# Group norm and attention on one core: loads split by columns, last probabilities kept in spent input, buffers moved by 32 bytes

## The chip, the core and the metric

One core of a Trainium2 chip runs the whole program. The time is the device time of that core in microseconds (us), from runs of the same kernel; less is better. The profile is one further execution, recorded by the hardware profiler.

## The reference

The input x has 16 images of 32 x 32 pixels with 512 channels, in float32. For every image (N = 1024 tokens, C = 512):

```
xn   = group_norm(x, 32 groups) * gamma + beta
q, k, v = xn @ wq + bq, xn @ wk + bk, xn @ wv + bv
attn = softmax(q @ k^T * C**-0.5)          # over the 1024 keys
out  = (attn @ v) @ wp + bp + x
```

## The kernel before, in words

**Algebra.** The weights are folded once, in a setup: A stands for wq and wk^T multiplied, M for wv and wp. So q k^T is computed as t against xn with t = A^T xn, and (attn v) wp as attn against v' = xn M. The biases bv, wp and bp make one row, out_bias, which is added to the residual x. Every matmul operand is split into a high and a low part (float32r), and each product is three matmuls: hi x hi, hi x lo, lo x hi (`product`, L780 to L791). Each matmul is 128 x 128 against 512 columns.

**One image on PE** (`image`, L896 to L918): two v tiles (24 matmuls), eight score tiles of the first half of the queries (h = 0, 12 matmuls each, xn stationary and t moving), four t chunks for the second half, six v tiles, eight score tiles of the second half, four output tiles of the first half (24 matmuls each, pt stationary and v moving, L871 to L873), four t chunks of the next image, four output tiles of the second half. The images 1 to 14 are a loop; the first and the last are written out.

**The softmax.** ACT copies a score tile to `score` (L451); DVE keeps a running maximum (top_part, L616); POOL reduces it over partitions (`top`, L334); DVE makes the shift and adds it to the eight tiles (`shifts`, L632); ACT takes the exp in place (L456), then writes the high part pt_hi (`pt_hi_parts`, L464), and DVE the low part pt_lo (`pt_lo_parts`, L637, by the helper at L524). POOL sums the exps (`totals`, L344) and reduces them over partitions (L352); DVE turns them into total_inv. `tile_out` (L652 to L658) scales an output tile and adds x_res, the residual in which POOL has added out_bias (`residual`, L322). For the second half the order is, on ACT, all eight exps (L507) and then pt_hi in four pairs; on DVE, tile_out 0, the eight shifts, tile_out 1 to 3, then pt_lo in pairs (L754 to L762). pt_hi waits at its start until the output tiles of the first half are done (s_o, L461), as these read the old pt.

**The loads.** SP issues all loads of x and of the weights, in the order written. An image of x comes in four quarters of 256 tokens (`load_quarter`, L232). Each quarter goes to one buffer [128, 1024]: partition i*32 + t holds the channels of block i (128 of 512) of token t, for the eight groups j of 32 tokens. The kernel issues one DMA for each i: 32 partitions, eight pieces of 512 bytes each. The first image goes to the free `score` buffer, the others to the two halves of x_blk. DVE transposes a quarter in 32 x 32 blocks to x_t (L533). In the loop a quarter is loaded once the quarter that had the buffer is transposed: quarters 2 and 3 of the next image after the transposes of its quarters 0 and 1. These transposes are placed by the table TRANSPOSED (L226). The rows of wq, wk and wv go to the partitions in the same permuted order (`load_weight`, L247), one DMA for each i, 32 partitions with four pieces of 2 KB. w_p is one DMA over 128 partitions. SP's order at the start: w_q, w_k, four quarters of x, w_v, w_p, three wide bias vectors, two quarters of image 1. ACT's queue loads gamma and beta, four rows with four pieces of 32 elements (128 bytes) each, and bv, four rows of 128 elements (512 bytes): L423 and L425.

**The setup chain behind w_p.** ACT writes wp_hi (L477), POOL wp_lo (L361); with these PE makes M. POOL then takes the root for rstd (L315), which DVE's norm and so xn wait for, and after it sums out_bias (L370 to L379). ACT waits for out_bias (L489) before it enters the first image.

**Addresses.** Buffers lie one after another, each rounded up to 32 bytes. In bytes within a partition: xn_hi 53088, xn_lo 69472, a_hi 85856, a_lo 94048, m_hi 102240, m_lo 110432 (all 32 past a multiple of 64), t_hi 145728, t_lo 153920, v_hi 162112, v_lo 178496, pt_hi 194880, pt_lo 211264 (all multiples of 64).

Of the kernel before, what the change touches and what calls it, by code (L numbers as in the profile page):

```python
# [8 lines left out]
ACT = mybir.ActivationFunctionType  # L9
# [4 lines left out]
P = 128  # L14
BANK = 512
# [4 lines left out]
def group_norm_attention(nc, x, gamma, beta, wq, bq, wk, bk, wv, bv, wp, bp, out):  # L20
# [28 lines left out]
    NQ = 4  # L49
    TQ = N // NQ  # L50
    assert NI == KC and SQ % CG == 0
    x_quarters = x.rearrange("b h w c -> b (h w) c").rearrange("b (q j t) (i r) -> b q i t j r", q=NQ, t=SQ, i=NI)
    out_rows = out.rearrange("b h w c -> b (h w) c").rearrange("b (t p) c -> b p t c", p=P)

    ctx = ExitStack()
    with ctx:
# [48 lines left out]
        with ExitStack() as setup:  # L105
# [3 lines left out]
                                              for n in ("wv_t_lo", "wv_t_hi", "wp_lo", "wp_hi"))  # L109
# [6 lines left out]
        (wq_t_hi, wq_t_lo), (wk_t_hi, wk_t_lo) = ([part[:, :, half * C:(half + 1) * C] for part in (xn_hi, xn_lo)]  # L116
                                                  for half in range(2))
        t_hi = sb("t_hi", [P, KC, BANK], F32R)
        t_lo = sb("t_lo", [P, KC, BANK], F32R)
# [67 lines left out]


        def starts(n, h=0):

            return h == 0 and isinstance(n, int) and n == 0
# [39 lines left out]
        def _(sp):  # L231
            def load_quarter(n, q):  # L232
                for i in range(NI):
                    sp.dma_start(quarter_of(n, q)[i * SQ:(i + 1) * SQ, :].rearrange("t (j r) -> t j r", r=P),  # L234
                                 x_quarters[n, q, i]).then_inc(s_xb[q], 16)

# [10 lines left out]
            def load_weight(w, dst, loaded):  # L247
                for i in range(NI):
                    sp.dma_start(dst[i * SQ:(i + 1) * SQ, :, :],  # L249
                                 w.rearrange("(i k a) n -> i a k n", i=NI, k=KC)[i]).then_inc(loaded, 16)  # L250

# [169 lines left out]
        def _(act):  # L421
# [36 lines left out]
            def pt_hi_parts(n, h, first, end):  # L458
                if first == 0 and end and not starts(n, h):

                    act.wait_ge(s_o, n * NT + h * TH)  # L461
                for m in range(first, end):
                    act.wait_ge(s_p, (n * NH + h) * NT + m + 1)
                    nc.scalar.activation(pt_hi[:, m, :], score[:, m, :], ACT.Copy).then_inc(s_pth, 1)  # L464

# [25 lines left out]
            def image(b, more):  # L491
                hi_part(b, "v", 0, 0)
                hi_part(b, "v", 0, 1)
                scores_out(b, 0)
                for j in range(KC):
                    hi_part(b, "t", 1, j)
                    exps(b, 0, *SHIFTED.get(("t", j), (0, 0)))
                for m in range(2, NT):
                    hi_part(b, "v", 0, m)
                    exps(b, 0, *SHIFTED.get(("v", m), (0, 0)))  # L500
                    pt_hi_parts(b, 0, *SPLIT_UP.get(("v", m), (0, 0)))
                scores_out(b, 1)
                if more:

                    act.wait_ge(s_work, use(b, "s", 1, NT - 1))
                    xn_split(b + 1)
                exps(b, 1, 0, NT)  # L507
                for j in range(KC):
                    pt_hi_parts(b, 1, 2 * j, 2 * j + 2)
                    if more:  # L510
                        hi_part(b + 1, "t", 0, j)
# [10 lines left out]
        def _(dve):  # L522
# [3 lines left out]
            def quarter_transpose(n, q):  # L526
                if q == 0 and not starts(n):

                    dve.wait_ge(s_rv, n * KC)
                dve.wait_ge(s_xb[q], (n + 1) * 16 * NI)  # L530
                blocks = quarter_of(n, q).rearrange("p (j k a) -> p k j a", k=KC, a=SQ)
# [102 lines left out]
            def pt_lo_parts(n, h, first, end):  # L634
                for m in range(first, end):
                    dve.wait_ge(s_pth, (n * NH + h) * NT + m + 1)
                    lo_part(pt_lo[:, m, :], score[:, m, :], pt_hi[:, m, :], s_ptl)  # L637

# [74 lines left out]
            def image(b, more):  # L713
# [41 lines left out]
                tile_shift(b, 1)  # L755
                shifts(b, 1, 0, NT)
                for i in range(1, TH):
                    tile_out(b, i)
                for j in range(KC):
                    pt_lo_parts(b, 1, 2 * j, 2 * j + 2)  # L760
                    if more:
                        split_lo_part(b + 1, "t", 0, j)  # L762
                if more:
                    for k in range(KC):
                        row_part(b + 1, k)
# [13 lines left out]
        def _(pe):  # L779
# [22 lines left out]
            def weight_transpose(u0, w, loaded):  # L802
                pe.wait_ge(loaded, 16 * NI)
                for j in range(KC):
# [50 lines left out]
            def out_tile(n, i, more):  # L855
# [7 lines left out]
                if i == TH - 1 and more:  # L863

                    pe.wait_ge(s_pw_in, n + 2)
                dst = o_ps[i % TH]
                for m in range(NT):
                    if i % TH == 0:
                        pe.wait_ge(s_ptl, (n * NH + h) * NT + m + 1)
                    queries = chunk(i % TH)  # L870
                    nc.tensor.matmul(dst, pt_hi[:, m, queries], v_hi[:, m, :], start=m == 0, stop=False)  # L871
                    nc.tensor.matmul(dst, pt_hi[:, m, queries], v_lo[:, m, :], start=False, stop=False)  # L872
                    last = nc.tensor.matmul(dst, pt_lo[:, m, queries], v_hi[:, m, :], start=False, stop=m == NT - 1)  # L873
                last.then_inc(s_o, 1)

# [71 lines left out]
```

## Time and profile before

| | us |
|---|---|
| median of 3 runs | 2180.49 (2180.29 to 2183.83) |
| the profiled execution, its own time | 2182.63 |
| its span in the profile | 2180.9 |
| PE busy with matmuls | 2153.6 (99% of the span) |
| DVE busy | 1434.9 (66%) |
| POOL busy | 829.6 (38%) |
| ACT busy | 672.7 (31%) |
| PE's first wait, for w_q | 8.4 |

Engines: PE is the matrix engine, DVE the vector engine, ACT the scalar engine, POOL GpSimd, SP the engine that issues DMAs here; SPq is SP's DMA issues. Matmuls overlap each other, so their duration (390 ns) is longer than the distance from one start to the next (227 ns): for the pace of PE the starts are what counts. "idle before" is how long an engine had been idle, with what ended it. Time in which an engine waits costs something only where the chain that ends last runs through it.

### The profile page before, as it was taken

Reading aid. Unit: us, or ns where it says so; the run is one execution under the profiler, and the core shown is the slowest. Engines: PE = TensorE matmul, PEld = TensorE weight load, DVE = VectorE, ACT = ScalarE, POOL = GpSimd, SP = SyncE. Lnnn points to the kernel's source line nnn. Section 1 sums busy time; section 2 is a strip of 40 time slices with the busy share of each in tenths; the row PEclk is TensorE's granted clock in tenths of the full one; section 3 lists DMA queues with packets and bytes.
Section 4 is the critical chain, followed back from the end, with each engine's and each line's share of the span. In section 5 each row is a group of like instructions: output and inputs, shape, how many; then the busy total and the mean of one; then the engine's idle time right before and its main releaser. Section 6 shows DMA issues by size and latency. Waiting matters only on the chain.

```text
span 2180.9 us, 28171 instructions
## 1 busy us (share of the span) xinstructions
PE 2153.6 (99%) x9425; PEld 1762.9 (81%) x9425; DVE 1434.9 (66%) x2280; ACT 672.7 (31%) x1113; POOL 829.6 (38%) x487
## 2 busy tenths in 40 slices
PE   6999999999999999999999999999999999999998
PEld 5788888888888888888888888888888888888886
DVE  6775675856668475774756758576684757748454
ACT  3241332414233132331413324142331323314231
POOL 3344343433433335332443434334333343324433
PEclk9999999999999999999999999999999999999999
DMA  7003021030302103021030210303021030210201
GB/s 169 20 15 102 1 73 43 29 86 0 96 19 58 58 5 101 10 63 53 14 101 0 72 43 29 86 0 96 19 58 58 5 101 10 63 53 10 68 0 59
DMA packets 109259, 106.03 MB, mean 49 GB/s; under 512 B 8492, under 2 KB 74032, under 8 KB 109232
## 3 DMA queue, kind: packets, MB, share of 16 engines
q1 hardware_dynamic: 109184, 105.68, 17.3%
q8 instruction: 15, 0.25, 0.0%
q14 instruction: 12, 0.10, 0.0%
q10 hardware_dynamic: 48, 0.01, 0.0%
HBM read 72.10 MB, written 33.55 MB: 48 GB/s over the span
## 4 chain that ended last, share of the span: by engine, by line
PE 94%; POOL 2%; issue 2%; SPq 1%; DMA 1%; ACT 0%; DVE 0%; POOLq 0%; ACTq 0%; DVEq 0%
PE psum L788 21%; PE psum L790 21%; PE psum L789 21%; PE psum L873 10%; PE psum L871 10%; PE psum L872 10%; SPq L234 1%; DMA w_p<-in_L_conv_wp_dram 1%; POOL total_part L344 0%; POOL bias_part L370 0%; POOL x_res L322 0%; SPq L249 0%; ACT score L456 0%; POOL out_bias L374 0%; PE psum L834 0%
## 5 line engine op out<-in xcount | busy, mean ns | idle before, releaser
L788 PE MATMUL psum<-t_hi,xn_hi 128*128 128x512 f32 x1024 | 406.4, 397 | 1.3 <-DVE v_lo L524 1.3
L790 PE MATMUL psum<-t_hi,xn_lo 128*128 128x512 f32 x1024 | 405.0, 396 | 0.0
L789 PE MATMUL psum<-t_lo,xn_hi 128*128 128x512 f32 x1024 | 405.0, 395 | 0.0
L871 PE MATMUL psum<-v_hi,pt_hi 128*128 128x512 f32 x1024 | 399.1, 390 | 4.5 <-DVE pt_lo L524 4.5
L873 PE MATMUL psum<-v_hi,pt_lo 128*128 128x512 f32 x1024 | 398.6, 389 | 0.0
L872 PE MATMUL psum<-v_lo,pt_hi 128*128 128x512 f32 x1024 | 398.6, 389 | 0.0
L322 POOL TENSOR_TENSOR x_res<-x_res,out_bias 128x512 f32<-128x512 f32 (+1 forms) x144 | 179.7, 1259 | 437.1 <-issue 233.8
L616 DVE TENSOR_TENSOR top_part<-top_part,score 128x512 f32<-128x512 f32 x192 | 169.3, 882 | 254.6 <-ACT score L451 253.1
L451 ACT ACTIVATE score<-psum 128x512 f32<-128x512 f32 x256 | 151.3, 599 | 481.3 <-PE psum L790 481.3
L344 POOL TENSOR_TENSOR total_part<-total_part,score 128x512 f32<-128x512 f32 x192 | 279.4, 1455 | 46.2 <-ACT score L456 31.5
L456 ACT ACTIVATE score<-score 128x512 f32<-128x512 f32 x256 | 157.5, 633 | 293.7 <-DVE score L632 293.7
L524 DVE TENSOR_TENSOR pt_lo<-score,pt_hi 128x512 fp32r<-128x512 f32 x256 | 243.0, 993 | 0.0
L788 PEld LDWEIGHTS psum<-t_hi,xn_hi 128*128 128x128 f32 x1024 | 192.4, 188 | 47.5 <-DVE v_lo L524 1.9
L790 PEld LDWEIGHTS psum<-t_hi,xn_lo 128*128 128x128 f32 x1024 | 192.3, 188 | 46.5
L871 PEld LDWEIGHTS psum<-v_hi,pt_hi 128*128 128x128 f32 x1024 | 192.2, 188 | 46.6 <-DVE pt_lo L524 4.6
L789 PEld LDWEIGHTS psum<-t_lo,xn_hi 128*128 128x128 f32 x1024 | 192.4, 188 | 45.6
L873 PEld LDWEIGHTS psum<-v_hi,pt_lo 128*128 128x128 f32 x1024 | 192.3, 188 | 40.2
L872 PEld LDWEIGHTS psum<-v_lo,pt_hi 128*128 128x128 f32 x1024 | 192.3, 188 | 39.9
L632 DVE TENSOR_TENSOR score<-score,shift 128x512 f32<-128x512 f32 x256 | 217.2, 904 | 1.1
L657 DVE SCALAR_TENSOR_TENSOR x_res<-psum,total_inv,x_res 128x512 f32<-128x512 f32 x128 | 93.6, 746 | 175.1 <-POOL x_res L322 108.9
L788 PE MATMUL psum<-xn_hi,a_hi 128*128 128x512 f32 x512 | 199.9, 390 | 2.7 <-DVE xn_lo L524 2.7
L788 PE MATMUL psum<-m_hi,xn_hi 128*128 128x512 f32 x512 | 200.7, 392 | 0.0
(101 smaller groups left out, 2995.0 us busy)
## 6 DMA issues: line engine op xcount, KB each, us to landing
x_res<-in_x_dram SPq DMA_DIRECT2D x128, 256.0 KB, 2.9
out_dram<-x_res SPq DMA_DIRECT2D x128, 256.0 KB, 2.1
x_blk<-in_x_dram SPq DMA_DIRECT2D x240, 128.0 KB, 2.9
score<-in_x_dram SPq DMA_DIRECT2D x16, 128.0 KB, 7.8
w_q<-in_L_conv_wq_dram SPq DMA_DIRECT2D x4, 256.0 KB, 4.8
w_k<-in_L_conv_wk_dram SPq DMA_DIRECT2D x4, 256.0 KB, 8.0
w_v<-in_L_conv_wv_dram SPq DMA_DIRECT2D x4, 256.0 KB, 8.4
w_p<-in_L_conv_wp_dram SPq DMA_DIRECT2D x1, 1024.0 KB, 11.4
```

What stands on the lines that cost most here:

```text
L322: last = nc.gpsimd.tensor_tensor(at, at, out_bias[:, first:end], ALU.add)
L344: nc.gpsimd.tensor_tensor(total_part[:], score[:, 0, :] if m == 1 else total_part[:], score[:, m, :], ALU.add).then_inc(s_sum, 1)
L456: nc.scalar.activation(score[:, m, :], score[:, m, :], ACT.Exp, scale=SCALE).then_inc(s_p, 1)
L524: nc.vector.tensor_tensor(dst, src, hi.bitcast(FP32), ALU.subtract).then_inc(signal, 1)
L616: nc.vector.tensor_tensor(top_part[:], score[:, 0, :] if m == 1 else top_part[:], score[:, m, :], ALU.max).then_inc(s_mx, 1)
L632: nc.vector.tensor_tensor(score[:, m, :], score[:, m, :], shift[:], ALU.add).then_inc(s_sub, 1)
L788: nc.tensor.matmul(dst, s_hi_, m_hi_, start=n == 0, stop=False)
L789: nc.tensor.matmul(dst, s_hi_, m_lo_, start=False, stop=False)
L790: last = nc.tensor.matmul(dst, s_lo_, m_hi_, start=False, stop=n == len(pairs) - 1)
L871: nc.tensor.matmul(dst, pt_hi[:, m, queries], v_hi[:, m, :], start=m == 0, stop=False)
L872: nc.tensor.matmul(dst, pt_hi[:, m, queries], v_lo[:, m, :], start=False, stop=False)
L873: last = nc.tensor.matmul(dst, pt_lo[:, m, queries], v_hi[:, m, :], start=False, stop=m == NT - 1)
```

## The change

Three things change.

1. `load_quarter` issues one DMA for each group j of 32 tokens (QJ = 8) in place of one for each channel block i: 128 partitions, one piece of 512 bytes each. `load_weight` issues one DMA for each k in place of each i: 128 partitions, one piece of 2 KB each. The semaphore counts that readers wait for follow.
2. A buffer t_offset of 32 bytes is put before t_hi, so t_hi, t_lo, v_hi, v_lo, pt_hi and pt_lo lie 32 bytes further on.
3. In the second half of the last image the probabilities are written over xn_hi and xn_lo, which are no longer needed once the last score product is done; so ACT waits for that product and not for the output tiles of the first half. Exps, shifts, pt_hi and pt_lo go in pairs there, and tile_out 1 to 3 come after pt_lo.

```diff
-    x_quarters = x.rearrange("b h w c -> b (h w) c").rearrange("b (q j t) (i r) -> b q i t j r", q=NQ, t=SQ, i=NI)
+    QJ = TQ // SQ
+    x_quarters = x.rearrange("b h w c -> b (h w) c").rearrange("b (q j t) (i r) -> b q j i t r", q=NQ, t=SQ, i=NI)
...
+        sb("t_offset", [P, 8])
         t_hi = sb("t_hi", [P, KC, BANK], F32R)
...
+        def final_half(n, h):
+            return h == NH - 1 and isinstance(n, int) and n == B - 1
+        def probs(n, h):
+            if final_half(n, h):
+                return [x[:].rearrange("p k (t q) -> p (k t) q", q=BANK) for x in (xn_hi, xn_lo)]
+            return pt_hi, pt_lo
...
             def load_quarter(n, q):
-                for i in range(NI):
-                    sp.dma_start(quarter_of(n, q)[i * SQ:(i + 1) * SQ, :].rearrange("t (j r) -> t j r", r=P),
-                                 x_quarters[n, q, i]).then_inc(s_xb[q], 16)
+                for j in range(QJ):
+                    sp.dma_start(quarter_of(n, q)[:, j * P:(j + 1) * P], x_quarters[n, q, j]).then_inc(s_xb[q], 16)
...
             def load_weight(w, dst, loaded):
-                for i in range(NI):
-                    sp.dma_start(dst[i * SQ:(i + 1) * SQ, :, :],
-                                 w.rearrange("(i k a) n -> i a k n", i=NI, k=KC)[i]).then_inc(loaded, 16)
+                for k in range(KC):
+                    sp.dma_start(dst[:, k, :],
+                                 w.rearrange("(i k a) n -> k i a n", i=NI, k=KC)[k]).then_inc(loaded, 16)
...
             def pt_hi_parts(n, h, first, end):
-                if first == 0 and end and not starts(n, h):
+                if first == 0 and end and final_half(n, h):
+                    act.wait_ge(s_work, use(n, "s", h, NT - 1))
+                elif first == 0 and end and not starts(n, h):
                     act.wait_ge(s_o, n * NT + h * TH)
...
-                exps(b, 1, 0, NT)
+                    exps(b, 1, 0, NT)
                 for j in range(KC):
+                    if not more:
+                        exps(b, 1, 2 * j, 2 * j + 2)
                     pt_hi_parts(b, 1, 2 * j, 2 * j + 2)
...
-                shifts(b, 1, 0, NT)
-                for i in range(1, TH):
-                    tile_out(b, i)
-                for j in range(KC):
-                    pt_lo_parts(b, 1, 2 * j, 2 * j + 2)
-                    if more:
+                if more:
+                    shifts(b, 1, 0, NT)
+                    for i in range(1, TH):
+                        tile_out(b, i)
+                    for j in range(KC):
+                        pt_lo_parts(b, 1, 2 * j, 2 * j + 2)
                         split_lo_part(b + 1, "t", 0, j)
+                else:
+                    shifts(b, 1, 0, 2)
+                    for j in range(KC):
+                        if j < KC - 1:
+                            shifts(b, 1, 2 * j + 2, 2 * j + 4)
+                        pt_lo_parts(b, 1, 2 * j, 2 * j + 2)
+                    for i in range(1, TH):
+                        tile_out(b, i)
```

The output tiles of the last half read `probs(n, h)` in place of pt_hi and pt_lo. The waits for a quarter and for a weight count 16 * QJ and 16 * KC in place of 16 * NI.

## Rows read from the trace of the kernel before

**Rows 1.** Page, part 4: shares of the chain that ended last, by engine.

```profile
PE 94%; POOL 2%; issue 2%; SPq 1%; DMA 1%; ACT 0%; DVE 0%; POOLq 0%; ACTq 0%; DVEq 0%
```

**Rows 2.** PE's timeline, one image: start us, us, engine line op out<-in.

```profile
995.61 0.40 PE L788 MATMUL psum<-t_hi,xn_hi 128*128 128x512 f32 x1
...
1018.01 0.39 PE L788 MATMUL psum<-xn_hi,a_hi 128*128 128x512 f32 x1
...
1028.92 0.39 PE L788 MATMUL psum<-m_hi,xn_hi 128*128 128x512 f32 x1
...
1034.36 0.28 PE L834 MATMUL psum<-mv,group_avg 128*128 128x4 f32 x2
...
1068.11 0.39 PE L871 MATMUL psum<-v_hi,pt_hi 128*128 128x512 f32 x1
...
1089.88 0.39 PE L788 MATMUL psum<-xn_hi,a_hi 128*128 128x512 f32 x1
```

**Rows 3.** PE's groups, shapes kept apart: xcount | busy us, mean ns.

```profile
L788 PE MATMUL psum<-t_hi,xn_hi 128*128 128x512 f32 x1024 | 406.4, 397 | 1.3 <-DVE v_lo L524 1.3
...
L871 PE MATMUL psum<-v_hi,pt_hi 128*128 128x512 f32 x1024 | 399.1, 390 | 4.5 <-DVE pt_lo L524 4.5
```

**Rows 4.** Timelines of ACT, POOL and ACT in the setup.

```profile
31.34 1.15 ACT L477 ACTIVATE wp_hi<-w_p 128x512 fp32r<-128x512 f32 x2 [4.24 <-DMA w_p<-in_L_conv_wp_dram]
...
39.02 1.50 POOL L315 TENSOR_TENSOR rstd<-g_var,minus_half 128x4 f32<-128x4 f32 x1 [1.47 <-DVE g_var L567]
...
72.67 1.08 ACT L439 ACTIVATE v_hi<-psum 128x512 fp32r<-128x512 f32 x2 [10.23 <-POOL out_bias L379]
```

**Rows 5.** The end: timelines of DVE, POOL, PE, then PE's waits.

```profile
2138.84 4.90 DVE L632 TENSOR_TENSOR score<-score,shift 128x512 f32<-128x512 f32 x8
...
2144.45 1.28 POOL L344 TENSOR_TENSOR total_part<-score 128x512 f32<-128x512 f32 x1 [7.17 <-ACT score L456]
...
2149.91 9.26 DVE L524 TENSOR_TENSOR pt_lo<-score,pt_hi 128x512 fp32r<-128x512 f32 x8
...
2173.80 3.76 POOL L322 TENSOR_TENSOR x_res<-x_res,out_bias 128x512 f32<-128x512 f32 x3 [7.70 <-issue]
...
2176.41 0.39 PE L873 MATMUL psum<-v_hi,pt_lo 128*128 128x512 f32 x1
...
PE psum L871 <- DVE pt_lo L524: 4.5, 5, 1.6
```

**Rows 6.** Page, parts 2, 3 and 6: packets, queues, two DMA issues.

```profile
DMA packets 109259, 106.03 MB, mean 49 GB/s; under 512 B 8492, under 2 KB 74032, under 8 KB 109232
...
q1 hardware_dynamic: 109184, 105.68, 17.3%
...
q10 hardware_dynamic: 48, 0.01, 0.0%
...
x_res<-in_x_dram SPq DMA_DIRECT2D x128, 256.0 KB, 2.9
...
x_blk<-in_x_dram SPq DMA_DIRECT2D x240, 128.0 KB, 2.9
```

**Rows 7.** Stretches: us, busy of each engine, PEclk, DMA share, GB/s.

```profile
16.00:18.00 2.00, 2.00 (x11) 1.65 (x10) 2.00 (x7) 0.00 (x0) 0.00 (x0) 1.00 1.22 204
...
30.00:32.00 2.00, 2.00 (x11) 2.00 (x11) 0.38 (x1) 0.66 (x2) 0.00 (x0) 0.52 1.05 385
...
1132.00:1134.00 2.00, 2.00 (x10) 1.61 (x9) 0.00 (x0) 0.15 (x1) 2.00 (x1) 1.00 0.80 214
```

**Rows 8.** SP's DMA issues at the start; DVE's x transposes in one image.

```profile
0.81 1.89 SPq L249 DMA_DIRECT2D w_q<-in_L_conv_wq_dram  x4
...
4.64 13.02 SPq L234 DMA_DIRECT2D score<-in_x_dram  x16
...
1005.55 1.42 DVE L533 STREAM_TRANSPOSE x_t<-x_blk 128x256 f32<-128x256 f32 x4
...
1022.35 1.41 DVE L533 STREAM_TRANSPOSE x_t<-x_blk 128x256 f32<-128x256 f32 x4
```

More of the change, by code:

```diff
@@ L463, in pt_hi_parts @@
                     act.wait_ge(s_p, (n * NH + h) * NT + m + 1)
-                    nc.scalar.activation(pt_hi[:, m, :], score[:, m, :], ACT.Copy).then_inc(s_pth, 1)
+                    nc.scalar.activation(probs(n, h)[0][:, m, :], score[:, m, :], ACT.Copy).then_inc(s_pth, 1)
             def setup_hi_parts(u0, dst, first=0, end=KC):
@@ L529, in quarter_transpose @@
                     dve.wait_ge(s_rv, n * KC)
-                dve.wait_ge(s_xb[q], (n + 1) * 16 * NI)
+                dve.wait_ge(s_xb[q], (n + 1) * 16 * QJ)
                 blocks = quarter_of(n, q).rearrange("p (j k a) -> p k j a", k=KC, a=SQ)
@@ L636, in pt_lo_parts @@
                     dve.wait_ge(s_pth, (n * NH + h) * NT + m + 1)
-                    lo_part(pt_lo[:, m, :], score[:, m, :], pt_hi[:, m, :], s_ptl)
+                    hi, lo = probs(n, h)
+                    lo_part(lo[:, m, :], score[:, m, :], hi[:, m, :], s_ptl)
             def totals(n, h):
@@ L802, in weight_transpose @@
             def weight_transpose(u0, w, loaded):
-                pe.wait_ge(loaded, 16 * NI)
+                pe.wait_ge(loaded, 16 * KC)
                 for j in range(KC):
@@ L866, in out_tile @@
                 dst = o_ps[i % TH]
+                hi, lo = probs(n, h)
                 for m in range(NT):
@@ L870, in out_tile @@
                     queries = chunk(i % TH)
[L871 to L874, printed above, removed]
+                    nc.tensor.matmul(dst, hi[:, m, queries], v_hi[:, m, :], start=m == 0, stop=False)
+                    nc.tensor.matmul(dst, hi[:, m, queries], v_lo[:, m, :], start=False, stop=False)
+                    end = nc.tensor.matmul(dst, lo[:, m, queries], v_hi[:, m, :], start=False, stop=m == NT - 1)
+                end.then_inc(s_o, 1)
             pe.wait_ge(s_const, 6)
```

## The prediction

> **What bounds the kernel now.** I read the chain of waits first: 94% of the span is PE, 2% POOL [rows 1]. Time can be won or lost where PE works, by making its work shorter, or at the few places where the chain leaves PE: the start and the end. The order of PE's instructions in one image shows phase after phase with no pause, but not at one spacing. The eight score tiles of the first half are 96 matmuls from 995.61 to 1018.01, 0.2333 us each; the four t chunks after them are 48 to 1028.92, 0.2273 us each; two v tiles are 24 to 1034.36, 0.2267 us each; four output tiles are 96 from 1068.11 to 1089.88, 0.2268 us each [rows 2]. All have 512 columns. The grouped view says the same: 397 ns for a matmul on t_hi, 390 ns for one on v_hi [rows 3].
>
> At the start the chain goes through SP's DMA issues and the load of w_p. ACT gets w_p at 31.34, after 4.24 us of waiting for this DMA; POOL's rstd follows at 39.02; POOL's serial sum of out_bias lets ACT write v_hi only at 72.67 [rows 4]. At the end it goes through POOL: the total begins at 2144.45, the last residuals run from 2173.80 for 3.76 us, and the last tile_out needs the last of them, while PE's last matmul starts at 2176.41 [rows 5].
>
> **Part 1, 32 bytes.** By the order and sizes of the buffers t, v and pt begin at a multiple of 64 bytes, and xn, a and m begin 32 bytes past one. A score matmul (xn against t) is the only one in the loop whose operands differ in that phase; v against pt agree, xn against a and m agree, and all these run at 0.2267 to 0.2273 us. The v tile has the same stationary xn as the score tile and differs in the moving operand alone, so xn by itself is not the cause. After the change all pairs agree, and I expect the score spacing to fall to that of the output tiles. There are 16 images x 16 tiles x 12 = 3072 score matmuls (three groups of 1024 [rows 3]): 3072 x (0.2333 - 0.2268) = 20 us. With the t and the v spacing in place of the output's it is 18 to 20.3; I widen it to 18 to 23 for what the ends of phases add. Nothing hides this, since PE rests nowhere in the loop. **Steady part: -20 us.**
>
> **Part 2, the loads.** A DMA of x had 32 outer rows on both sides before, one of a weight too. After, the destination has 128 partitions, but the source is (i t) r or (i a) n: its outermost count is i = 4, and i cannot be merged with t or a, because the strides don't fit. Does such a DMA run on 16 engines or on 4? The trace holds a count. There are 8492 packets under 512 B [rows 6]. The gamma and beta loads of ACT's queue are 32 pieces of 128 B, the only data pieces that small. SP's queue has 528 DMAs (128 loads and 128 stores of x_res, 240 of x_blk, 16 of score, 12 + 1 of the weights, 3 of the wide vectors), with outer counts of 32 or 128; at 16 small completion packets each that is 8448. There remain 8492 - 8448 - 32 = 12 for ACT's three DMAs, 4 each. ACT's queue agrees: 48 packets are 16 + 16 + 4 pieces of data and 12 more [rows 6]. The source of each of those three has an outermost count of 4. So a DMA with a count of 4 was spread over 4 engines, one with 32 or 128 over 16. No row shows 4 against 128, and the bounds are 4 and 16 engines. I take 4: the rows nearest to it have the same outermost count on the source side, and a source walked in four outer steps cannot be dealt out in 16 equal shares of them.
>
> The Trainium skill's page "DMA: Bandwidth & Descriptors", section "Why a DMA increments its semaphore by 16 and not by 1", says that the engine count is the largest up to 16 that divides the outermost count of both sides. The counts of rows 6 agree with it where both sides are equal; by it the sum is the one for four engines.
>
> Price of 4 engines. From 30 to 32 us, while w_p's 2 KB pieces move, 16 engines carry 385 GB/s, 24.1 GB/s each; with x's 512 B pieces 214 GB/s at a share of 0.80 is 268 at full share, 16.7 GB/s each [rows 7]. Each of the four carries a quarter of w_q, w_k and w_v (0.786 MB, 32.6 us), a quarter of x's first image (0.524 MB, 31.4 us) and behind them a sixteenth of w_p (2.7 us): 66.7 us. To this come 0.8 us before the first issue [rows 8] and 2.1 us for the way of one transfer (an x_res load lands 2.9 us after its issue [rows 6], 0.7 of it moving). w_p then lands at 69.6 instead of 31.3: **start +38 us.** Everything later in the setup hangs on it: wp_hi, wp_lo, POOL's rstd behind wp_lo, norm, out_bias. x (at 56) and w_v (at 67) land before it, so the order of the waits stays and the whole shifts. Bounds: x at 24.1 GB/s too gives +29; x as in the crowded stretch (204 GB/s, 12.8 each [rows 7]) gives +48.
>
> SP issues 16 more x DMAs in front of w_v and w_p, 16 x 0.47 = 8 us by the pace of w_q's four (1.89 us). It had to wait for room in the queue anyway (13.02 us for 16 of x [rows 8]), so behind four slow engines they cost nothing.
>
> In the loop a quarter is 8 issues, 2 us more of SP's time, which SP has. Its 0.52 MB take 7.9 us on four engines. The tightest place is quarter 3: it may be loaded when DVE has transposed quarter 1, at 1005.55 + 1.42, and is wanted at 1022.35 [rows 8]. 1007.0 + 7.9 + 2 = 1016.9, at the slow rate 1019.2: 3 us to spare, the other quarters have more. So the loads cost nothing there; with that cover gone t_lo would come late and PE would stop.
>
> **Part 3, the last half.** PE's five waits for pt_lo, 4.5 us, go, and PE ends near 2172. But the end is POOL's. Its total starts at 2144.45, after an idle of 7.17 that follows its own reduction, and what comes after it, up to the last residual, has only POOL's order in it [rows 5]. The exps keep ahead of it: in pairs, with a shift of 0.61 us on DVE and as much on ACT for each exp and each pt_hi, the last exp ends near 2149.5, and POOL's seventh addition begins near 2153. The tile_outs 1 to 3 move behind pt_lo, to about 2150; their x_res loads land near 2157, and POOL wants them at 2173.80. ACT's new wait (for the last score product) is over when ACT reaches it. DVE's pt_lo beside POOL's additions took 9.26 us for 8 [rows 5]; now other additions are beside it. I take 0, bounds -1 and +1.
>
> **Sum.** +38 - 20 + 0 = +18. The profiled execution took 2182.6 us (span 2180.9), 2.1 above the median of the runs; its like after the change is 2200.6, and against the median of 2180.5 it is 2199 (2198.5, rounded up).
>
> **The rivals.** A is the sum above; its own range is 2186 to 2210 (+29 - 23 to +48 - 18).
>
> B: four engines, and the offset does nothing, because the score spacing belongs to something else in t or in the pair. For it: the trace has just one mismatched pair. Against it: the three other products of the loop (t, v, output) are all at the lower spacing. Time: 2180.5 + 38 = 2219.
>
> C, on the other side: 16 engines after all. Then the loads gain: with 32 partitions for each DMA the queue moved 204 GB/s, with w_p's 128 it moved 385 [rows 7]. SP's issuing becomes the limit, 8 + 32 + 4 + 1 issues at 0.47 us are 21 us, w_p lands near 27, 4 us earlier, and the time is 2180.5 - 4 - 20 = 2156. It decides from six engines up: there the start loses less than 20 us. For it speaks the rate, against it the count of completions.
>
> The skill's page "SBUF — State Buffer", section "Door 1: The DMA port swizzle", says that 32 partitions reach 8 of the 16 ports and 128 reach all; the rates of rows 7 agree. By that rule alone the time would be C's.
>
> D: 16 engines and no effect of the offset: 2176.5.
>
> **How the numbers follow.** Chances: A 0.70, B 0.12, C 0.14, D 0.04. The forecast is A's, 2199. Leaving out C, D and the outer edges, 2186 to 2228 holds 8 in 10. A measurement of this kernel can tell about 0.2% (4.4 us) from no change. Faster: C and part of D, 0.16. Same: the rest of D, and A with engines faster than any row shows, 0.05. Slower: 0.79.
>
> **What would show it.** Right: PE's wait for w_q grows from 8.4 to about 14 us; the first 60 us move 60 to 100 GB/s; w_p lands near 70; packets under 512 B fall to about 6300 (512 + 12 DMAs with 4, 260 with 16), where C would have 12,600; score matmuls 0.2268 us apart; no wait for pt_lo at the end and the same rows of POOL last. Wrong: over 250 GB/s in the first 10 us (C), or score matmuls still at 0.2333 (B).

## The result and the profile after

The changed kernel takes 2198.79 us (median of 6 runs, 2197.97 to 2201.05); the kernel before, run beside it, 2181.66 (6 runs, 2180.29 to 2183.83). The ratio is 1.0079, with a 95% interval of 1.0067 to 1.0092: 17.1 us slower. The forecast was 2199, the range 2186 to 2228.

The profiled execution took 2198.91 us, its span is 2197.2. First the page of the kernel after (parts 1, 2, 4, 5 and 6). The helper that records the matmuls, L788 to L790 before, is L813 to L815 now; the output tiles, L871 to L873 before, are L897 to L899.

```profile
PE 2134.5 (97%) x9425; PEld 1764.9 (80%) x9425; DVE 1443.3 (66%) x2280; ACT 672.8 (31%) x1113; POOL 828.3 (38%) x487
...
PEclk9899999999999999999999999999999999999999
...
DMA packets 107067, 106.02 MB, mean 48 GB/s; under 512 B 6300, under 2 KB 71840, under 8 KB 107040
...
PE 90%; POOL 3%; issue 2%; SPq 2%; DMA 1%; DVE 1%; ACT 1%; POOLq 0%; DVEq 0%; ACTq 0%
...
L813 PE MATMUL psum<-t_hi,xn_hi 128*128 128x512 f32 x1024 | 399.9, 390 | 3.8 <-DVE v_lo L540 3.8
...
L897 PE MATMUL psum<-v_hi,pt_hi 128*128 128x512 f32 x992 | 385.9, 389 | 0.0
...
x_blk<-in_x_dram SPq DMA_DIRECT2D x480, 64.0 KB
```

PE is busy for 19 us less than before (2153.6), and yet the span is 16.3 longer: its work became shorter and its waiting grew more. The chain says where: PE's share falls from 94% to 90%, SP's issues have 2% where they had 1%, POOL 3% where it had 2% [rows 1]. The granted clock has a slice of 0.8 near the start (the second digit), which it did not have. The small packets are exactly 6300, against 8492 [rows 6]. A score matmul takes 390 ns against 397 [rows 3].

PE's timeline of the kernel after: the start, and one image of the loop.

```profile
14.61 3.65 PE L832 MATMUL psum<-ident,w_q 128*128 128x128 f32 x16 [14.61 <-DMA w_q<-in_L_conv_wq_dram]
25.10 3.68 PE L832 MATMUL psum<-ident,w_k 128*128 128x128 f32 x16 [6.84 <-DMA w_k<-in_L_conv_wk_dram]
...
64.15 3.68 PE L832 MATMUL psum<-ident,w_v 128*128 128x128 f32 x16 [23.12 <-DMA w_v<-in_L_conv_wv_dram]
...
1024.18 0.39 PE L813 MATMUL psum<-t_hi,xn_hi 128*128 128x512 f32 x1
...
1045.94 0.39 PE L813 MATMUL psum<-xn_hi,a_hi 128*128 128x512 f32 x1
...
1095.39 0.39 PE L897 MATMUL psum<-v_hi,pt_hi 128*128 128x512 f32 x1
...
1117.15 0.39 PE L813 MATMUL psum<-xn_hi,a_hi 128*128 128x512 f32 x1
...
1155.23 0.39 PE L813 MATMUL psum<-t_hi,xn_hi 128*128 128x512 f32 x1
```

In the loop 96 score matmuls now take 1045.94 - 1024.18 = 21.76 us, 0.2267 each; before it was 22.40 and 0.2333 [rows 2]. The 96 output matmuls from 1095.39 to 1117.15 take 21.76 too: one spacing for both. From one image's score start to the next it is 1155.23 - 1024.18 = 131.05 us; before it was 1128.05 - 995.61 = 132.44, with the first of these in rows 2 and the other here, from the trace of the kernel before:

```profile
1128.05 0.40 PE L788 MATMUL psum<-t_hi,xn_hi 128*128 128x512 f32 x1
```

At the start PE waits 14.6 us for w_q (8.4 before), 6.8 for w_k and 23.1 for w_v. SP's own timeline shows why these come late. (Start us, us, queue, line, op, out<-in, count.)

```profile
0.81 2.85 SPq L260 DMA_DIRECT2D w_q<-in_L_conv_wq_dram  x4
3.70 9.62 SPq L260 DMA_DIRECT2D w_k<-in_L_conv_wk_dram  x4
13.37 32.80 SPq L246 DMA_DIRECT2D score<-in_x_dram  x32
46.21 3.21 SPq L260 DMA_DIRECT2D w_v<-in_L_conv_wv_dram  x4
```

The 32 DMAs of x take 32.80 us to issue where 16 took 13.02 [rows 8]: SP is not slower, it waits for room in a queue that drains slowly. Each quarter of 8 DMAs reaches DVE 6.3 us behind the one before it. The stretches of the kernel after, in the columns of rows 7:

```profile
8.00:14.00 6.00, 0.00 (x0) 0.00 (x0) 0.00 (x0) 0.00 (x0) 0.00 (x0) 1.00 0.26 100
26.00:32.00 6.00, 6.00 (x24) 5.04 (x23) 3.53 (x7) 2.39 (x4) 0.00 (x0) 1.00 0.29 83
...
50.00:60.00 10.00, 0.00 (x0) 0.00 (x0) 6.55 (x16) 0.00 (x0) 0.00 (x0) 0.50 0.79 192
```

From 8 to 14 us the weights' 2 KB pieces move at 100 GB/s at a DMA share of 0.26, from 26 to 32 the 512-byte pieces of x at 83 GB/s and 0.29. A share of about a quarter, held steadily, is four busy engines of 16. Only from 50 us on, when w_p and the wide vectors with their 128 outer rows are under way, does the share rise to 0.79. PE works in none of the 10 us before 60, its granted clock there is 0.50, that is 1.2 GHz, so w_v's transposes start at the lower of the two levels. They take 3.68 us, no longer than w_k's 3.68 between 25 and 29 us, where the granted clock is 1.00, so no cost of it shows at this place.

ACT's timeline of the kernel after gives the two marks of the setup that answer to rows 4.

```profile
66.76 1.15 ACT L491 ACTIVATE wp_hi<-w_p 128x512 fp32r<-128x512 f32 x2 [25.09 <-DMA w_p<-in_L_conv_wp_dram]
...
108.75 1.08 ACT L450 ACTIVATE v_hi<-psum 128x512 fp32r<-128x512 f32 x2 [10.87 <-POOL out_bias L390]
```

Cut at these marks, the span difference of 16.3 us falls into three parts. The table has the same cuts for these two and eight of the kernels below; the other four have a section of their own. "w_p" is the start of ACT's wp_hi, "v_hi" the start of ACT's first v_hi, "top" the start of DVE's last top_part; "steady" runs from v_hi to top, "end" from top to the end of the span.

| kernel | w_p | v_hi | steady | end | span |
|---|---|---|---|---|---|
| before | 31.34 | 72.67 | 2055.40 | 52.83 | 2180.9 |
| after | 66.76 | 108.75 | 2035.49 | 52.96 | 2197.2 |
| offset alone | 31.05 | 72.67 | 2034.27 | 53.36 | 2160.3 |
| loads alone | 66.73 | 108.47 | 2055.79 | 52.14 | 2216.4 |
| last half alone | 29.95 | 71.92 | 2056.95 | 53.33 | 2182.2 |
| after, with the old loads | 31.38 | 73.66 | 2033.89 | 53.85 | 2161.4 |
| loads of x alone | 48.94 | 90.15 | 2056.41 | 52.14 | 2198.7 |
| loads of weights alone | 52.70 | 94.35 | 2056.49 | 53.06 | 2203.9 |
| twice the issues | 29.57 | 70.88 | 2055.39 | 52.13 | 2178.4 |
| old loads, other order | 27.71 | 70.26 | 2034.20 | 54.24 | 2158.7 |

After against before: the setup +36.1, the steady part -19.9, the end +0.1. With the old loads in their old order w_p comes anywhere from 29.57 to 31.38, and the ends without the new last half run from 52.13 to 53.36 here, so a difference of 1 us in one cell proves nothing.

The end of the kernel after, first DVE's timeline, then POOL's, to be held against rows 5.

```profile
2162.27 3.48 DVE L648 TENSOR_TENSOR score<-score,shift 128x512 f32<-128x512 f32 x2
2165.67 6.86 DVE L540 TENSOR_TENSOR xn_lo<-score,xn_hi 128x512 fp32r<-128x512 f32 x4
...
2193.89 0.75 DVE L674 SCALAR_TENSOR_TENSOR x_res<-psum,total_inv,x_res 128x512 f32<-128x512 f32 x1 [0.47 <-POOL x_res L333]
```

```profile
2160.29 1.51 POOL L355 TENSOR_TENSOR total_part<-score 128x512 f32<-128x512 f32 x1 [6.82 <-issue]
2161.94 10.04 POOL L355 TENSOR_TENSOR total_part<-total_part,score 128x512 f32<-128x512 f32 x6
...
2179.88 3.25 POOL L363 PARTITION_ALL_REDUCE total_part<-total_part  x1 [6.21 <-issue]
2190.11 3.70 POOL L333 TENSOR_TENSOR x_res<-x_res,out_bias 128x512 f32<-128x512 f32 x3 [6.98 <-issue]
```

POOL's order is the old one. Its total begins 16.05 us after the last top_part (16.38 before) and its last residuals 29.82 after that (29.35 before). PE's last matmul starts at 2189.50, 45.26 after the last top_part, where before it was 48.34: PE ends 3 us earlier, and the end does not move, since the last tile_out at 2193.89 waits for POOL. The two ends lay close together before: PE's last matmul started at 2176.41 and the last tile_out at 2177.65, with a wait of 0.48 us for POOL.

PE's waits in the kernel after (us in all, times, longest us):

```profile
PE psum L813 <- DVE v_lo L540: 3.8, 2, 2.1
...
PE psum L897 <- DVE xn_lo L540: 2.0, 3, 0.7
```

The low part of the probabilities is xn_lo now. Of 4.5 us of waiting for it [rows 5] 2.0 are left: DVE's seventh and eighth shift take 3.48 us for two (912 ns is the mean of one shift over the kernel, and the four ahead of POOL's additions took 2.50) while POOL's additions run, so the last two exps and what follows them come late. And one wait has grown: for v_lo in image 0, from 1.3 [rows 3] to 3.8.

### The profile page after: what moved, and what is told of

It is laid out like the page before. It is cut to its first block, busy times and chain, and to the rows that moved or that the text cites. A ratio compares the mean times of both kernels' runs of the same rounds, so it can differ in the third digit from the quotient of the medians.

```text
span 2197.2 us, 28843 instructions
## 1 busy us (share of the span) xinstructions
PE 2134.5 (97%) x9425; PEld 1764.9 (80%) x9425; DVE 1443.3 (66%) x2280; ACT 672.8 (31%) x1113; POOL 828.3 (38%) x487
## 4 chain that ended last, share of the span: by engine, by line
PE 90%; POOL 3%; issue 2%; SPq 2%; DMA 1%; DVE 1%; ACT 1%; POOLq 0%; DVEq 0%; ACTq 0%
PE psum L813 20%; PE psum L815 20%; PE psum L814 20%; PE psum L898 10%; PE psum L899 10%; PE psum L897 10%; SPq L246 1%; DMA w_p<-in_L_conv_wp_dram 1%; SPq L260 1%; POOL total_part L355 0%; POOL x_res L333 0%; POOL bias_part L381 0%; DVE score L648 0%; POOLq L57 0%; POOL row L367 0%
## 5 line engine op out<-in xcount | busy, mean ns | idle before, releaser
L813 PE MATMUL psum<-t_hi,xn_hi 128*128 128x512 f32 x1024 | 399.9, 390 | 3.8 <-DVE v_lo L540 3.8
L815 PE MATMUL psum<-t_hi,xn_lo 128*128 128x512 f32 x1024 | 398.5, 389 | 0.0
L814 PE MATMUL psum<-t_lo,xn_hi 128*128 128x512 f32 x1024 | 398.4, 389 | 0.0
L897 PE MATMUL psum<-v_hi,pt_hi 128*128 128x512 f32 x992 | 385.9, 389 | 0.0
L898 PE MATMUL psum<-v_lo,pt_hi 128*128 128x512 f32 x992 | 385.9, 389 | 0.0
L899 PE MATMUL psum<-v_hi,pt_lo 128*128 128x512 f32 x992 | 385.9, 389 | 0.0
L632 DVE TENSOR_TENSOR top_part<-top_part,score 128x512 f32<-128x512 f32 x192 | 176.1, 917 | 229.8 <-ACT score L462 228.1
L540 DVE TENSOR_TENSOR pt_lo<-score,pt_hi 128x512 fp32r<-128x512 f32 x248 | 233.9, 986 | 0.0
L813 PEld LDWEIGHTS psum<-t_hi,xn_hi 128*128 128x128 f32 x1024 | 192.3, 188 | 44.0 <-DVE v_lo L540 4.6
L815 PEld LDWEIGHTS psum<-t_hi,xn_lo 128*128 128x128 f32 x1024 | 192.2, 188 | 40.0
L897 PEld LDWEIGHTS psum<-v_hi,pt_hi 128*128 128x128 f32 x992 | 186.2, 188 | 38.7
L898 PEld LDWEIGHTS psum<-v_lo,pt_hi 128*128 128x128 f32 x992 | 186.2, 188 | 38.7
L899 PEld LDWEIGHTS psum<-v_hi,pt_lo 128*128 128x128 f32 x992 | 186.2, 188 | 38.6
L813 PE MATMUL psum<-xn_hi,a_hi 128*128 128x512 f32 x512 | 199.6, 390 | 2.7 <-DVE xn_lo L540 2.7
L813 PE MATMUL psum<-m_hi,xn_hi 128*128 128x512 f32 x512 | 200.5, 392 | 0.0
```

The lines of the kernel that those rows point to most:

```text
L540: nc.vector.tensor_tensor(dst, src, hi.bitcast(FP32), ALU.subtract).then_inc(signal, 1)
L632: nc.vector.tensor_tensor(top_part[:], score[:, 0, :] if m == 1 else top_part[:], score[:, m, :], ALU.max).then_inc(s_mx, 1)
L813: nc.tensor.matmul(dst, s_hi_, m_hi_, start=n == 0, stop=False)
L814: nc.tensor.matmul(dst, s_hi_, m_lo_, start=False, stop=False)
L815: last = nc.tensor.matmul(dst, s_lo_, m_hi_, start=False, stop=n == len(pairs) - 1)
L897: nc.tensor.matmul(dst, hi[:, m, queries], v_hi[:, m, :], start=m == 0, stop=False)
```

## The experiments

Unless told otherwise each starts from the kernel before and keeps its offsets, loads and last half where the edit doesn't change them. The lines of the matmul helper and of the output tiles move by one or two in kernels with added lines.

### The three parts alone

**The offset alone.**

```diff
+        sb("t_offset", [P, 8])
         t_hi = sb("t_hi", [P, KC, BANK], F32R)
```

> The kernel before with the 32-byte offset alone. The account of the prediction (the score spacing follows the phase of the two operands): score matmuls 0.2267 us apart instead of 0.2333, 20 us less, some 2162. Rival (the lower spacing after the change came with the loads or with the last half): spacing and time as before, 2182.

Measured: 2160.92 us, ratio 0.9900 (0.9885 to 0.9915), 21.5 us less. The steady part is 21.1 shorter, setup and end are as before. By the starts of its matmuls a first-half score phase is at 0.2267 us a matmul.

**The loads alone.** The loops over j and over k, and the counts of the waits, as in the change; the rest as before.

> The kernel before with the new loads of x and of the weights alone. The account: four engines, w_p lands at 67 instead of 31, everything behind it shifts by 35 to 36 us, packets under 512 B are 6300, the time is about 2217 and the score spacing stays at 0.2333. Rival (the start is late for another reason, as the offset): about 2182.

Measured: 2218.34 us, ratio 1.0166 (1.0151 to 1.0182), 35.9 us more. w_p comes at 66.73, and the steady part is 2055.79 against 2055.40: 240 DMAs more for x in the loop, each on four engines, cost it nothing that shows.

**The last half alone.** `probs`, the pairs, and tile_out 1 to 3 behind pt_lo; offsets and loads as before.

> The kernel before with the new order of the last half alone. The account: PE's waits for pt_lo (4.5 us) go, but POOL's chain from the last top_part to the end stays, and with it the time, 0 within 1 us. Rival (PE's waits counted): 4 us less.

Measured: 2183.46 us, ratio 1.0005 (0.9996 to 1.0014), +1.0 us: no difference that this can tell. PE's waits and POOL's timeline of this kernel:

```profile
PE psum L897 <- DVE xn_lo L540: 1.1, 2, 0.7
```

```profile
2145.76 1.31 POOL L355 TENSOR_TENSOR total_part<-score 128x512 f32<-128x512 f32 x1 [7.62 <-ACT score L467]
2147.21 10.05 POOL L355 TENSOR_TENSOR total_part<-total_part,score 128x512 f32<-128x512 f32 x6
...
2175.17 3.70 POOL L333 TENSOR_TENSOR x_res<-x_res,out_bias 128x512 f32<-128x512 f32 x3 [7.05 <-issue]
```

PE waits 1.1 us in place of 4.5, and POOL's last residuals still begin 29.4 us after its total begins (29.35 before). What PE wins is off the chain. POOL's own additions, which are on it, became slower. From the first of the seven to the residual behind them it is 11.6 us here, 11.8 in the kernel after, 11.7 with the old loads and 12.8 with the loads in another order, where the first addition alone took 3.56 us. In the ten kernels of this study with the old last half, the one before among them, it is 10.4 to 11.0. Other DVE work stands beside these additions now; that this is what slows them was not tried by itself.

The three differences are -21.5, +35.9 and +1.0, in sum +15.4; all three parts together gave +17.1. Runs of one kernel differ by 2 to 4 us, so a gap of 1.7 between sums of three medians can't be told from noise.

**The change, with the old loads.** Against the kernel after:

```diff
-                for j in range(QJ):
-                    sp.dma_start(quarter_of(n, q)[:, j * P:(j + 1) * P], x_quarters[n, q, j]).then_inc(s_xb[q], 16)
+                for i in range(NI):
+                    sp.dma_start(quarter_of(n, q)[i * SQ:(i + 1) * SQ, :].rearrange("t (j r) -> t j r", r=P),
+                                 x_quarters[n, q, i]).then_inc(s_xb[q], 16)
```

and the same for the weights.

> The changed kernel with the loads of before put back. The account: offset and last half remain, 2182 - 20 = 2162, faster than both kernels. Rival (parts do not add up, as the gain of the offset rests on the late start): 2175 or more.

Measured: 2163.17 us, ratio 0.9912 (0.9897 to 0.9927). Against the kernel after that is 2198.79 - 2163.17 = 35.6 us for the loads, the same within the noise as from the other side (35.9). Against the offset alone (2160.92) the last half is 2.3 us more here, with runs that do not overlap (2163.03 to 2163.39 against 2159.78 to 2162.05): with +1.0 from the last half alone it is more likely a small loss than nothing.

### What the 32 bytes do

Rival B held that the score spacing belongs to something else. The offset alone spoke against it, but left open whether it is the place of t, or the difference in phase between the two operands. Four kernels tell these apart. In the last column is where xn (with a and m), t (with v) and pt begin, in bytes modulo 64.

| kernel | edit | xn, t, pt |
|---|---|---|
| 64 bytes ahead of t_hi | `sb("t_offset", [P, 16])` | 32, 0, 0 |
| xn moved | `sb("x_offset", [P, 8])` ahead of x_res | 0, 32, 32 |
| all on 64 | the line above and `sb("t_offset", [P, 8])` ahead of t_hi | 0, 0, 0 |
| pt apart | `sb("t_offset", [P, 8])` ahead of t_hi, `sb("pt_offset", [P, 8])` ahead of pt_hi | 32, 32, 0 |

> Before with 64 bytes in place of 32, so t, v and pt move but keep their phase, and xn and t still differ. Account (phase of the pair): score spacing 0.2333, time as before, 2182. Rival (any other place of t will do): 0.2267, 2162.

> Before with 32 bytes in front of x_res: every matmul operand moves, xn, a and m now on multiples of 64, t, v and pt 32 past one. Account: the pair xn and t still differs, 0.2333, 2182. Rival (t is quick wherever it starts 32 past a multiple of 64): 0.2267, 2162.

> Before with 32 bytes in front of x_res and 32 in front of t_hi: all operands on multiples of 64. Account: every pair agrees, all at 0.2267, 2162. Rival (operands 32 past a multiple are the quick ones): score at 0.2333 or more, 2182.

> Before with the offset of 32 and another 32 bytes in front of pt_hi, so that xn and t agree and v and pt differ. Account: score at 0.2267, output tiles at 0.2333, 20 us won and 20 lost, 2182. Rival (only score products are hit): 2162.

Measured: 2182.12 us with 64 bytes (1.0002, 0.9991 to 1.0013), 2180.50 with xn moved (0.9994, 0.9983 to 1.0006), 2158.70 with all on 64 (0.9891, 0.9862 to 0.9920), 2181.49 with pt apart (0.9995, 0.9983 to 1.0006). PE's groups with shapes kept apart, one fence for each kernel, in this order (count | busy us, mean ns | idle before):

```profile
L789 PE MATMUL psum<-t_hi,xn_hi 128*128 128x512 f32 x1024 | 406.4, 397 | 1.6 <-DVE v_lo L525 1.6
```

```profile
L789 PE MATMUL psum<-t_hi,xn_hi 128*128 128x512 f32 x1024 | 406.5, 397 | 1.1 <-DVE v_lo L525 1.1
```

```profile
L790 PE MATMUL psum<-t_hi,xn_hi 128*128 128x512 f32 x1024 | 399.8, 390 | 1.4 <-DVE v_lo L526 1.4
L873 PE MATMUL psum<-v_hi,pt_hi 128*128 128x512 f32 x1024 | 399.3, 390 | 3.4 <-DVE pt_lo L526 3.2
```

```profile
L873 PE MATMUL psum<-v_hi,pt_hi 128*128 128x512 f32 x1024 | 406.4, 397 | 3.6 <-DVE pt_lo L526 3.6
...
L790 PE MATMUL psum<-t_hi,xn_hi 128*128 128x512 f32 x1024 | 399.9, 391 | 1.3 <-DVE v_lo L526 1.3
```

Moving t by 64 bytes changes nothing. Moving xn to 0 while t goes to 32 keeps the score matmul at 397 ns. With all at 0 it is 390, as it is with both at 32. With pt at 0 and v at 32 the cost leaves the score matmuls and appears at the output tiles: 397 ns there, 391 in the score. So it is the pair that matters, not t, not a buffer's absolute address, and not one kind of product. With pt apart 96 output matmuls take 1088.17 - 1065.78 = 22.39 us, 0.2332 each; with operands in phase they start every 0.2267. Shifts by less than 32 bytes were not tried.

Two of these kernels also show how narrowly POOL holds the end. Their last tile_out, all on 64 first, then pt apart:

```profile
2153.45 0.75 DVE L659 SCALAR_TENSOR_TENSOR x_res<-psum,total_inv,x_res 128x512 f32<-128x512 f32 x1 [1.62 <-PE psum L875]
```

```profile
2176.47 0.75 DVE L659 SCALAR_TENSOR_TENSOR x_res<-psum,total_inv,x_res 128x512 f32<-128x512 f32 x1 [3.73 <-PE psum L875]
```

Here it waits for PE and not for POOL. From the last top_part to the end of the span it is 52.0 us in the first and 54.7 in the second, whose output matmuls are the slow ones.

### What the loads do

**Each load's share.** First the loop of `load_quarter` alone, then that of `load_weight` alone, as in the change.

> Before with the new loads of x alone, weights as before. Account: 0.52 MB on each of four engines at 16 to 20 GB/s is about 26 to 31 us where 2 MB took 10 before, so w_p 15 to 20 us later, about 2199. Rival (512 B pieces or their count do the harm): all of the 36 us here, 2217.

> Before with the new loads of the weights alone. Account: the other part of the 36 us, w_p 15 to 20 us later, about 2199, although each DMA has the same pieces of 2 KB and the same number as before. Rival (pieces of 512 B do the harm): 2182 or less.

Measured: x alone 2201.44 us (1.0089, 1.0069 to 1.0109), weights alone 2204.33 (1.0102, 1.0082 to 1.0122). The page's count of packets of the first, with a stretch of it (columns of rows 7), and the count of the second:

```profile
DMA packets 107211, 106.02 MB, mean 48 GB/s; under 512 B 6444, under 2 KB 71984, under 8 KB 107184
...
14.00:20.00 6.00, 5.96 (x32) 4.90 (x31) 3.40 (x8) 2.34 (x5) 0.00 (x0) 1.00 0.29 83
```

```profile
DMA packets 109115, 106.03 MB, mean 48 GB/s; under 512 B 8348, under 2 KB 73888, under 8 KB 109088
```

The small packets are what four engines give for just the DMAs that were changed: with x, 512 DMAs of 4 and 272 of 16, 2048 + 4352, and 44 of ACT's queue, is 6444; with the weights, 12 of 4 and 516 of 16, and 44, is 8348. From 14 to 20 us x moves at 83 GB/s at a share of 0.29, with the weights loaded in the old way. The weights cost their part although their pieces (2 KB) and the number of their DMAs are the old ones, so neither small pieces nor more DMAs are the cause there. Both times lie 2 to 5 us above the 2199 that was expected. So the engine count is set by each DMA's own access pattern, and its outermost count of 4 on the source side is enough although the destination has 128 partitions.

By the Trainium skill's page "DMA: Bandwidth & Descriptors", section "Why a DMA increments its semaphore by 16 and not by 1", the count is the largest number up to 16 that divides the outermost counts of both sides; for 4 against 128 that is 4. These counts agree, and they are the unequal case that rows 6 did not have.

w_p came 17.6 us later by x's loads and 21.4 by the weights', in sum 39.0, while together they cost 35.4. Part of the difference shows where four-engine DMAs run beside wide ones: with the weights alone w_k is there at 27.37, 12.8 us after w_q, since x, on all 16 engines, moves beside it; in the kernel after it is 10.5 (14.61 to 25.10). That the other engines' traffic is what slows it was not tried by itself.

**More issues, 16 engines.** To part the engine count from the number of DMAs: the DMAs of x cut in two, 8 for each quarter as in the change, but still 32 partitions each.

```diff
                 for i in range(NI):
-                    sp.dma_start(quarter_of(n, q)[i * SQ:(i + 1) * SQ, :].rearrange("t (j r) -> t j r", r=P),
-                                 x_quarters[n, q, i]).then_inc(s_xb[q], 16)
+                    for g in range(2):
+                        sp.dma_start(quarter_of(n, q)[i * SQ:(i + 1) * SQ, g * TQ * 2:(g + 1) * TQ * 2].rearrange("t (j r) -> t j r", r=P),
+                                     x_quarters[n, q, i][:, g * 4:(g + 1) * 4, :]).then_inc(s_xb[q], 16)
```

> Before with each x DMA cut in two along j: as many DMAs per quarter as in the change (8), but 32 outer rows on both sides. Account (the engines, not the number of DMAs, make the start late): 16 engines, packets under 512 B rise to 12,588, w_p lands within 3 us of 31.3, 2182 to 2185. Rival (the number of issues in front of w_p): w_p some 10 us later or more, over 2190.

Measured: 2181.29 us, ratio 0.9996 (0.9986 to 1.0007); w_p at 29.57. The page's packets and SP's timeline of this kernel:

```profile
DMA packets 113355, 106.04 MB, mean 49 GB/s; under 512 B 12588, under 2 KB 78128, under 8 KB 113328
```

```profile
4.63 15.16 SPq L236 DMA_DIRECT2D score<-in_x_dram  x32
```

12,588 small packets are 256 DMAs of x more, at 16 each. 32 issues of x take 15.16 us (0.47 each) and not 32.80: twice as many DMAs cost nothing, on 16 engines.

**Old loads, other order.** What a faster start would look like. Blocks 0 and 1 of a DMA series lie in partitions 0 to 63, blocks 2 and 3 in 64 to 127. The old loads take them in order; this kernel (the change with the old loads) alternates.

```diff
-                for i in range(NI):
+                for i in (0, 2, 1, 3):
```

in `load_quarter` and in `load_weight`.

> The changed kernel with the loads of before in the order i = 0, 2, 1, 3, so that neighbouring DMAs write to different halves of the partitions. Account (the old loads are held at 204 to 209 GB/s by the partitions that one DMA reaches, and DMAs in flight overlap): w_p lands up to 5 us earlier, 2158 to 2163. Rival (16 engines keep in step, one DMA after the other): as with the old loads, 2163.

Measured: 2158.42 us, ratio 0.9889 (0.9873 to 0.9906) against the kernel before, 23.6 us less; the change with the old loads was 19.3 less. Stretches and page (part 6, with the us to landing) of the change with the old loads, then of this kernel:

```profile
8.00:14.00 6.00, 4.61 (x25) 4.24 (x26) 2.77 (x4) 2.66 (x5) 0.00 (x0) 1.00 1.12 202
14.00:20.00 6.00, 5.96 (x32) 4.94 (x31) 5.52 (x14) 2.40 (x5) 0.00 (x0) 1.00 1.23 193
20.00:26.00 6.00, 6.00 (x28) 4.89 (x27) 5.78 (x14) 1.20 (x2) 0.00 (x0) 1.00 1.13 206
...
score<-in_x_dram SPq DMA_DIRECT2D x16, 128.0 KB, 8.0
```

```profile
8.00:14.00 6.00, 5.22 (x33) 4.65 (x31) 3.68 (x6) 3.93 (x8) 0.00 (x0) 1.00 1.14 231
14.00:20.00 6.00, 6.00 (x27) 4.94 (x28) 5.96 (x15) 1.44 (x4) 0.00 (x0) 1.00 1.21 238
20.00:26.00 6.00, 5.89 (x30) 4.69 (x29) 6.00 (x15) 1.48 (x3) 0.00 (x0) 1.00 1.06 266
...
score<-in_x_dram SPq DMA_DIRECT2D x16, 128.0 KB, 6.8
```

At about the same DMA share (1.14, 1.21, 1.06 against 1.12, 1.23, 1.13) the queue moves 231, 238 and 266 GB/s in place of 202, 193 and 206. A DMA of x lands after 6.8 us, not 8.0, and w_p comes at 27.71, 3.7 earlier, the lowest of all kernels here. The rates of the old order vary by themselves: the eight traces that have it, with DMAs as before, show 202 to 209, 193 to 225 and 206 to 219 GB/s in these stretches, 7.4 to 8.1 us to landing, and w_p between 29.66 and 31.38. The new order lies outside all of these ranges, by 22, 13 and 47 GB/s and by 1.9 us for w_p, but it has one trace. Its four runs (2156.66 to 2160.41) lie below all four of the change with the old loads (2163.03 to 2163.39). This is the fastest version of the study by its median, beside all on 64 (2158.70) and the offset alone (2160.92); the intervals of the three overlap, so which of them is best is not settled.

The Trainium skill's page "SBUF — State Buffer", section "Door 1: The DMA port swizzle", has partitions 0 to 63 on eight of the 16 ports and 64 to 127 on the other eight, which would let neighbouring DMAs overlap in the new order. The Trainium skill's page "DMA: Bandwidth & Descriptors", section "Rules for kernel authors", says that two transfers to disjoint partition halves serialize, so that one need not bother. Here the rate in the new order is 6 to 21% above the highest of the eight traces in each of the three stretches, which speaks against the second for a train of 128 to 256 KB DMAs with 32 partitions each. That it is the ports is argued, not shown.

## Why the prediction was right

The forecast was right in sign, size and cause, and rival A's condition, four engines and an offset that works, holds. That it came within 1 us is luck in part. Errors within the price of the loads cancel (see the table below), the offset gives up to 1.5 us more than forecast and a stall that was not foreseen takes it back, and the forecast stands on 2180.5 us for the kernel before, which measured 2181.66 beside the kernel after: +18 was forecast and +17.1 found. Step by step:

**What bounds the kernel.** Right. The offset alone gave -21.5 us through PE's spacing, and the last half alone, which frees PE of 3.4 us of waits, gained nothing at the end.

**Part 1.** Forecast -20 us (18 to 23) from a spacing of 0.2268; found 0.2267, and 21.1 to 21.5 us where the offset stands without the new loads. The difference between two images, 132.44 - 131.05 = 1.39, times 16 is 22.2. Of this the score is 3072 x 0.00667 = 20.5; the rest lies with the t chunks (0.2273 to 0.2267 each) and the ends of phases. The argument by which it was chosen, that xn against t is the only mismatched pair, is borne out by four more placements.

**Part 2, the engine count.** Right: 4, where both 4 and 16 were open, to the exact number of 6300 packets. The argument from ACT's three small DMAs held.

**Part 2, the price.** Near in sum, since errors of opposite sign cancel in part: +35.4 us on w_p for +38.

| term | forecast us | found us | from |
|---|---|---|---|
| w_q there | 13.8 | 14.6 | PE's wait |
| w_k behind w_q | 10.9 | 10.5 | 14.61 to 25.10 |
| x, four quarters | 31.4 | 25.2 | 25.10 to 50.27, DVE's transposes |
| w_v behind x | 10.9 | 13.9 | 50.27 to 64.15 |
| w_p behind w_v | 2.7 | 2.6 | 64.15 to 66.76 |
| w_p there | 69.6 | 66.8 | ACT |

The x term was mis-sized. It took 16.7 GB/s for each engine from the stretch of rows 7 in which the loop's x is loaded; four engines carry 83 GB/s, 20.8 each. That row was measured on DMAs of 32 partitions on 16 engines; whether its lower rate comes from the 32 partitions or from 16 engines at work at once was not parted. The w_v term was too small by 3 us: it runs beside w_p and the wide vectors, whose 128 rows are spread over all engines, which may be why; that was not tried by itself. The same shows for w_k in the kernel with the new weight loads alone. What hung on w_p moved with it as forecast: v_hi is 41.3 us behind it before and 42.0 after.

**Part 2, the issues.** Right: 16 more for the first image cost nothing, as twice the issues on 16 engines showed too; and the loop, where quarter 3 was said to have 3 us to spare, loads in time (steady 2055.79 against 2055.40).

**Part 3.** Right that the end is POOL's and that PE's gain does not reach it: forecast 0 (-1 to +1), found +0.1 in the cut of the full change and +1.0 alone, with an interval that holds zero. The offset alone and the change with the old loads differ by 2.3, so 0 was on the low side. The step that failed is "now other additions are beside it. I take 0": POOL's seven additions take 11.6 to 12.8 us with the new last half and 10.4 to 11.0 without, some 1 us on the chain, where the forecast put nothing. From the start of POOL's total to its last residuals it is 29.4 to 30.4 us in the four kernels with the new last half and 27.8 to 29.4 in the ten without. The row before that the forecast leaned on, 29.35, is the highest of those ten. Wrong in another step: "PE's five waits for pt_lo, 4.5 us, go, and PE ends near 2172". Three waits, 2.0 us, stay, and PE ends 3 us earlier, not 4.5. What failed is the 0.61 us for each shift: the last two run beside POOL's additions and take 3.48 us for two, and the last exps come behind them. Off the chain, it cost nothing.

**What was not foreseen.** A stall of PE in image 0: waits for v_lo are 3.8 us where the kernel before had 1.3 [rows 3]. They are the likely reason that the steady part gained 19.9 and not 21.1 to 21.5 as in the offset alone and in the change with the old loads. These two have 2.2 and 2.3 us of this wait. The loads alone start as late as the kernel after and have 1.7, so the late start by itself does not make it either. Why the two together give 3.8 stays open.

**The rivals.** B falls by the five kernels with other placements of the buffers. C and D fall by the packets and by 83 to 100 GB/s between 8 and 40 us. C's rate was nevertheless half true: neighbouring DMAs that write other halves of the partitions do go faster, but the way there was the order of the old loads, and against the change with the old loads it is worth some 4 us.

## What to carry to other kernels

Ahead of reshaping a DMA, look at the outermost count of both sides and not just at how many partitions it writes: a count of 4 on the source held it on four engines, and a DMA share of 0.25 to 0.3 while a queue is full is the sign of it. Where PE is busy for 99% of the span, compare the spacing from start to start between products of the same shape; 3% between two of them was a matter of 32 bytes. An engine that waits less is worth nothing if the last instruction waits for another: the shorter waits of the last half did not bring the end forward, since POOL's order set it, and work moved beside POOL's can make POOL slower.

## What the runs showed of the hardware

- Two float32r operands of a matmul whose start addresses differ by 32 modulo 64 bytes cost 0.2333 us per 512 columns in place of 0.2267, whichever of the two is moved and for score and output products alike; both at 32 is as good as both at 0. A shift by 64 changes nothing.
- Four DMA engines carry 83 GB/s in pieces of 512 bytes and some 100 GB/s in pieces of 2 KB, and 1 MB on four engines takes 10.5 us alone and 12.8 to 13.9 while wide DMAs run beside it.
- Between 8 and 26 us, neighbouring DMAs of 32 partitions moved 231 to 266 GB/s when they alternate between the lower and the upper half of the partitions (one trace), and 193 to 225 when they don't (eight traces).
- The trace shows GpSimd idle for some 6 us ahead of its reductions over partitions at the end and for 7 behind the last: 6.21 and 6.98 around the one of 3.25 us in the kernel after, 13.2 us for which it names no cause, more than its six additions take. In all fourteen traces it is 5.7 to 6.2 us ahead of each and 6.6 to 7.7 behind the last. The profile's spans on this engine are rough, so part of the idle time may belong to the reduction itself.
